# Audio tower on one core: the token stage with all its turns by transposing transfers and three convolution banks, and another order inside an attention slot

## Chip, core, metric

One core of a Trainium2 chip runs the whole program in one launch. The metric is the device time of that core in microseconds (us), the median of several executions. The engines named here: TensorE (PE, with its weight loads PEld), VectorE (DVE), ScalarE (ACT), GpSimd (POOL) and SyncE (SP), which here only issues transfers.

## What is computed

Three stages follow each other. The token stage makes 2048 tokens of 1024 numbers (16 tiles of 128 channels), the attention stage adds a 32-head latent attention to them, and the feed-forward stage adds a linear layer with a low-rank expert part.

```python
h = conv1d(x, conv_in_w, pad=3)                    # x (16, 64, 2048), 7 taps, 128 channels
h = gelu(groupnorm1(h))
h = conv1d(h, dw_w, stride=2, pad=2, groups=128) + dw_b   # 5 taps for each channel
h = conv1d(h, pw_w)                                # 128 x 128, one tap
h = gelu(groupnorm1(h))                            # 16 tiles of 128 x 1024

n = layernorm(h)
q_c = rmsnorm(n @ w_qa, g_qa)                      # 384 latents for the queries
kv  = n @ w_kva                                    # 128 latents and 64 rope numbers
k_c, k_rope = rmsnorm(kv[:, :128], g_kva), rope(kv[:, 128:])
q = q_c @ w_qb                                     # 32 heads, 128 + 64 (rope) each
p = softmax(q . [k_c @ w_kvb_key, k_rope] * scaling)     # 128 x 128 in each tile and head
h = h + (p @ (k_c @ w_kvb_value)) @ w_o

h = h + layernorm(h) @ W_base.T + b_base + experts(layernorm(h))
```

Every product wants float32 accuracy and runs in float16: an operand is split into a high half and a low half, and a product is three products (high by high, high by low, low by high). So each operand costs one pass for the high half (mostly ACT) and one for the low half (mostly DVE, "value minus high half").

## The kernel before

**Token stage** (`token_phase`, lines 108 to 640). The work is written out engine by engine: each engine runs its own list in order, and semaphores join them. A function `body(i, p, ok)` is the list of one iteration; a tile b passes through five iterations, and `AHEAD, MID, HID, PROJ, TAIL = -2, 1, 2, 3, 4` say by how many iterations each step trails the convolution of its tile. In iteration i:

- PE: convolution piece 0 of tile i (12 products of 512 columns into one of two banks `conv_ps`); the statistics product (`stat_ps`, L609), which spreads the group norm sums of tile i-1 (first norm) and tile i-2 (second norm) over the partitions; transposes of the normalised tile i-3 (`turn_ps`, L569) between the convolution pieces 1, 2 and 3; the projection of tile i-3 to q and kv in two pieces; transposes of the latents of tile i-4 (L631, L633, L640); the pointwise product of tile i-1 (`pw_ps`).
- ACT: copies of the four convolution pieces to `y1`, high halves of the turned tile (`ht_h`), the first gelu (`g1`, L261) of tile i-1, the second gelu (`resid`), the float16 copy of input tile i+2 (`x_high`), squares for the rms norm, high halves of the latents, the normalised tile `hid` (L303).
- DVE: sums for the second group norm (`bn2`, L479) at the head of the iteration, the copy of the statistics (`s`, L485), the latents' first steps, low halves of the turned tile, the sums of the first norm (`bn1`, L403), the five taps of the depthwise convolution (`dw`, L419 and L423, five instructions over SBUF alone), the sums of the layer norm (`bn3`), the low halves of the latents out of `turn_ps`.
- POOL: eleven short linked steps that turn `s` into the scale and bias `c12` of both group norms (L337 to L344), then the rms scales of tile i-4, the layer norm scales of tile i-2, and last the low half of input tile i+2 (`x_low`, L326).
- SP: the input loads.

The cycle through an iteration is: statistics product (PE), `s` (DVE), group norm steps (POOL), first gelu (ACT), taps (DVE), sums of `bn1` and `bn2` (DVE), next statistics product.

**Attention stage** (`attention_phase`, lines 706 to 1119) has 32 rounds of one group of four heads and one of two halves of the tokens, four slots (128-token tiles) in each: 128 slots. Slot s = 4t + j does on PE: scores (`s_ps`, L1051 to L1058, the rope part from `zt`), latents of the slot before (`av_ps`, L1093 to L1095, from the turned probabilities `turned`), the rope queries of the next slot, the queries of the next round (`qp_ps`), in slots 1 to 3 one of three pieces of a weight product (`prod_ps`, "products", which the last rounds don't have), and the outputs of the slot before (`out_ps`, 24 products of 512 columns). The softmax chain of a slot runs beside: maxima (DVE, `mx`), exponentials (ACT, L851), reciprocal and normalisation (DVE), high half (ACT) and low half (DVE) into `halves`, one transposing transfer by SP into `turned`. SP issues the rope turn `zt` of slot s+1 ahead of `turned` of slot s. The next heads' weights (928 KB) are loaded by ACT's queue at the head of its round's list (L819); ACT comes to that line when it has taken slot 3 of the round before.

**Feed-forward stage** (`ffn_phase`, from line 1126): not touched.

## Time and profile before

| what | value |
| --- | --- |
| median of 3 runs | 2093.45 us (2093.0 to 2094.6) |
| the profiled execution: its own time | 2096.29 us |
| its span | 2094.5 us |
| token stage | 0.7 to 458.9 us |
| attention stage | 458.9 to 1857.9 us |
| feed-forward stage | 1857.9 to 2094.5 us |
| PE busy over the span | 1924.3 us (92%) |
| DVE, ACT, POOL busy | 1310.3, 755.6, 286.4 us |

Busy shares over the span mix three stages with different limits, so they are to be read stage by stage. PE's busy time is modelled and runs a little over into the next product; where it stands in a window at nearly the whole window, PE does not wait. POOL works only in the token stage and beside the feed-forward stage.

### The profile page before, as it was taken

The page shows a single profiled execution, that of the slowest core. Times are in us where ns is not written, and L with a number is a line of the kernel's source. Part 1 is how long each engine was busy: PE and PEld are TensorE (multiplying, and loading weights), DVE is VectorE, ACT ScalarE, POOL GpSimd, SP SyncE. Part 2 cuts the span into 40 slices and gives each one's busy share as a digit, 9 for nine tenths or more (in the row PEclk, how much of TensorE's full clock was granted, in tenths as well). Part 3 has the DMA queues.
Part 4 walks back from the last instruction along what each step waited for, and adds up shares of the span by engine and source line. Part 5 has one row for each costly group of instructions (what it writes and reads, how often), then busy time and mean ns, then how long its engine had stood idle before and what let it go on. Part 6 is the DMA issues. An engine that isn't in the chain of part 4 may idle for free. (4 is left out here: it accounts for less than half of the span.)

```text
span 2094.5 us, 33517 instructions
## 1 busy us (share of the span) xinstructions
PE 1924.3 (92%) x11794; PEld 1064.8 (51%) x11794; DVE 1310.3 (63%) x2805; ACT 755.6 (36%) x2051; POOL 286.4 (14%) x612
## 2 busy tenths in 40 slices
PE   4788888768999999999999999999999999959999
PEld 1344445444555555555555555555555555525554
DVE  2667677635666666666566665666666666665554
ACT  3444544324333333333333333333333333332221
POOL 2355554320000000000000000000000000023332
PEclk9899999879999999999999999999999999989999
DMA  5112211002332232222322223222232212243332
GB/s 139 41 41 50 53 41 39 19 26 73 75 57 57 57 63 63 55 57 57 75 57 56 54 55 73 56 57 57 66 58 57 39 38 44 41 134 81 82 81 71
DMA packets 250668, 125.27 MB, mean 60 GB/s; under 512 B 240272, under 2 KB 240528, under 8 KB 248336
## 3 DMA queue, kind: packets, MB, share of 16 engines
q1 hardware_dynamic: 246192, 94.71, 21.7%
q10 hardware_dynamic: 4320, 28.51, 4.4%
q8 instruction: 94, 1.54, 0.3%
q14 instruction: 62, 0.51, 0.1%
HBM read 56.07 MB, written 8.39 MB: 31 GB/s over the span
## 5 line engine op out<-in xcount | busy, mean ns | idle before, releaser
L1073 PE MATMUL out_ps<-m_h,ot_h 128*128 128x512 f16 x1024 | 388.2, 379 | 4.1 <-DVE ot_l L872 4.1
L1075 PE MATMUL out_ps<-m_h,ot_l 128*128 128x512 f16 x1024 | 388.1, 379 | 0.0
L1074 PE MATMUL out_ps<-m_l,ot_h 128*128 128x512 f16 x1024 | 388.1, 379 | 0.0
L922 DVE SCALAR_TENSOR_TENSOR resid<-out_ps,resid 128x512 f32<-128x512 f32 x256 | 177.0, 691 | 285.4 <-PE out_ps L1075 281.4
L787 ACT ACTIVATE ot_h<-av_ps 128x512 f16<-128x512 f32 x128 | 76.4, 597 | 744.2 <-PE av_ps L1095 744.2
L1264 POOL MEMSET fpower<- 128x1 f32 x1 | 0.1, 99 | 1405.0 <-POOLq L706 1405.0
L851 ACT ACTIVATE prob<-s_ps,nmx 128x128 f32<-128x128 f32 x512 | 180.1, 372 | 5.7 <-DVE nmx L948 5.7
L1073 PEld LDWEIGHTS out_ps<-m_h,ot_h 128*128 128x128 f16 x1024 | 100.2, 98 | 129.7 <-issue 13.4
L1074 PEld LDWEIGHTS out_ps<-m_l,ot_h 128*128 128x128 f16 x1024 | 100.2, 98 | 129.2 <-issue 18.6
L1075 PEld LDWEIGHTS out_ps<-m_h,ot_l 128*128 128x128 f16 x1024 | 100.2, 98 | 120.9
L943 DVE TENSOR_REDUCE mx<-s_ps 128x4 f32<-128x512 f32 x128 | 88.5, 691 | 74.8 <-PE s_ps L1058 74.8
L872 DVE SCALAR_TENSOR_TENSOR ot_l<-av_ps,ot_h 128x512 f16<-128x512 f32 x128 | 88.5, 691 | 70.3 <-ACT ot_h L787 70.3
L872 DVE SCALAR_TENSOR_TENSOR halves<-prob,halves 128x512 f16<-128x512 f32 x128 | 88.6, 692 | 46.4 <-ACT halves L787 46.4
L851 ACT ACTIVATION_READ_ACCUMULATOR prob<-s_ps,nmx 128x1 f32 x512 | 109.3, 213 | 0.0
L1008 PE MATMUL qp_ps<-qct_h,wp_h 128*128 128x512 f16 x378 | 104.8, 387 | 0.0
L1008 PE MATMUL qp_ps<-qct_h,wp_l 128*128 128x512 f16 x378 | 102.7, 381 | 0.0
L1008 PE MATMUL qp_ps<-qct_l,wp_h 128*128 128x512 f16 x378 | 102.1, 379 | 0.0
L787 ACT ACTIVATE halves<-prob 128x512 f16<-128x512 f32 x128 | 80.6, 630 | 51.3 <-DVE prob L956 51.3
L1377 PE MATMUL fout<-wb_l,fht_h 128*128 128x512 f16 x256 | 97.3, 380 | 0.0
L1377 PE MATMUL fout<-wb_h,fht_h 128*128 128x512 f16 x256 | 97.3, 380 | 0.0
L1377 PE MATMUL fout<-wb_h,fht_l 128*128 128x512 f16 x256 | 97.1, 379 | 0.0
L1051 PE MATMUL s_ps<-kct_h,qp_h 128*128 128x128 f16 x512 | 92.4, 219 | 0.4 <-DVE qp_l L872 0.4
(239 smaller groups left out, 4011.7 us busy)
## 6 DMA issues: line engine op xcount, KB each, us to landing
wide<-heads_in ACTq DMA_DIRECT2D x30, 928.0 KB, 5.3
wide<-x_in SPq DMA_DIRECT2D x32, 512.0 KB, 6.3
tower_out<-result SPq DMA_DIRECT2D x16, 512.0 KB, 2.6
stage<-wb_in SPq DMA_DIRECT2D x8, 512.0 KB, 8.5
resid<-wqk_in SPq DMA_DIRECT2D x1, 2304.0 KB, 12.5
zt<-z SPq DMA_TRANSPOSE x128, 2.4
turned<-halves SPq DMA_TRANSPOSE x128, 3.0
wide<-heads_in SPq DMA_DIRECT2D x2, 928.0 KB, 5.3
```

The lines of the kernel that those rows point to most:

```text
L787: act.activation(out, src, ACT.Copy, scale=scale).then_inc(done, 1)
L851: act.activation(prob[:, h, :], s_ps[:, h * P:(h + 1) * P], ACT.Exp, bias=nmx[:, h:h + 1], scale=EXP_SCALE, accum_out=rsum[:, h:h + 1]).th ...
L872: dve.scalar_tensor_tensor(out=out, in0=src, scalar=scale, in1=high, op0=ALU.mult, op1=ALU.subtract).then_inc(done, 1)
L922: dve.scalar_tensor_tensor(out=resid[:, at], in0=out_ps[hf][:, :], scalar=1.0 / (O_S * M_S), in1=resid[:, at], op0=ALU.mult, op1=ALU.add). ...
L943: dve.tensor_reduce(mx[:, :], s_ps[:, :].rearrange("p (h n) -> p h n", h=HEADS), AX.X, ALU.max).then_inc(max_step, 1)
L1008: last = pe.matmul(bank[:, :], w[:, bass.ds(side, 1), k, j, :].rearrange("p a n -> p (a n)"), q[:, k, bass.ds(tok, CHUNK)], start=n == 0, ...
L1051: pe.matmul(out[h], q_h[h], k_h, start=h == 0, stop=False)
L1073: pe.matmul(out_ps[hf][:, :], ot_h[:, h, :], m_h[:, at], start=h == 0, stop=False)
L1074: pe.matmul(out_ps[hf][:, :], ot_h[:, h, :], m_l[:, at], start=False, stop=False)
L1075: last = pe.matmul(out_ps[hf][:, :], ot_l[:, h, :], m_h[:, at], start=False, stop=h == HEADS - 1)
L1264: pool.memset(power[:, :], -0.5).then_inc(powered, 1)
L1377: pe.matmul(out_ps[p][hf][:, :], h[p][:, k, :], w[:, k, hf * CHUNK:(hf + 1) * CHUNK], start=k == 0 and n == 0, stop=False)
```

## The change

In the token stage:

- The lags become -1, 1, 2, 3, 4 and a sixth, LOW = 5; there is one iteration more.
- PE makes no transposes. ACT writes the normalised tile and its high half to SBUF (`hid2`), DVE the low half beside it, and SP turns both with one transposing transfer of 128x2048 into `ht`. The latents are treated alike: high halves by ACT (iteration TAIL), low halves by DVE one iteration later (LOW), then two transposing transfers by SP (128x1024 into `lat`, 128x256 into the same).
- The freed bank is a third convolution bank, and the projection is one piece behind convolution piece 3.
- `bn2` and its aggregation move from the head of the next iteration to the end of DVE's list. `bn3` stands ahead of the last two `bn1` sums.
- POOL computes the low half of input tile i+1 right behind the group norm steps, instead of tile i+2 behind the layer norm steps. ACT's high half of that tile stands between copies 0 and 1.
- The first input tile is loaded head first (1032 columns), and the convolution of its first two pieces waits for the head alone.
- The rms scales take seven linked steps, not eight; the group norm's eleven steps lose one wait.

In the attention stage the latents product of slot s moves to the end of slot s itself, and the outputs of slot s-1 to before the queries. SP issues `zt` of slot s behind `turned` of slot s-1. ACT's and DVE's halves of `av_ps` stand at the end of the slot, and the output additions of DVE ahead of the queries' low halves. The heads' loads keep their place at the head of ACT's round.

The core of the diff:

```diff
-    AHEAD, MID, HID, PROJ, TAIL = -2, 1, 2, 3, 4
+    AHEAD, MID, HID, PROJ, TAIL, LOW = -1, 1, 2, 3, 4, 5
-        conv_ps = [pb("conv_ps0"), pb("conv_ps1")]
-        stat_ps, turn_ps = pb("stat_ps"), pb("turn_ps")
+        conv_ps = [pb("conv_ps0"), pb("conv_ps1"), pb("conv_ps2")]
+        stat_ps = pb("stat_ps")
...
+                if ok(PROJ):
+                    b = i - PROJ
+                    sp.wait_ge(hid_lo, b + 1)
+                    need(sp, proj_done, b, B)
+                    sp.dma_start_transpose(ht[:, :, :], hid2[:, :]).then_inc(hid_turned, 16)
+                if ok(LOW):
+                    b = i - LOW
+                    sp.wait_ge(lat_lo, b * 2 + 2)
+                    sp.dma_start_transpose(lat[:, 0:8, b * P:(b + 1) * P],
+                                           lat2[:, :, :].rearrange("p a n -> p (a n)")).then_inc(lat_turned, 16)
...
             def body(i, p, ok):
-                if isinstance(i, int) and i == 0:
-                    x_low(1, 1)
                 if ok(MID) or ok(HID):
                     group_norms(i)
+                if ok(AHEAD) and i >= 0:
+                    x_low(i - AHEAD)
                 if ok(TAIL):
                     latent_scales(i - TAIL)
                 if ok(HID):
                     layer_norm(i - HID)
-                if ok(AHEAD) and (not isinstance(i, int) or i >= 0):
-                    x_low(i - AHEAD, p)
...
+                if ok(PROJ):
+                    b = i - PROJ
+                    dve.wait_ge(hid_hi, b + 1)
+                    need(dve, hid_turned, b * 16, B * 16)
+                    low(hid2[:, D:2 * D], hid[:, :], LN_S, hid2[:, 0:D], hid_lo)
+                if ok(LOW):
+                    latents_low(i - LOW)
                 if ok(TAIL):
                     take_latents(i - TAIL)
-                if ok(PROJ):
-                    hidden_low(i - PROJ, 0)
...
             def turn_rope(s):
-                wait_apart(sp, sp_passed, (z_lo, s + 1))
+                waits = [(z_lo, s + 1)]
...
             turn_rope(0)
-            turn_rope(1)
             turn_prob(0)
-            with sp.Fori(1, ROUNDS * QUAD - 1) as s:
-                turn_rope(s + 1)
+            with sp.Fori(1, ROUNDS * QUAD) as s:
+                turn_rope(s)
                 turn_prob(s)
...
                     scores(now, j, operands)
-                    if behind[0]:
-                        latents(*behind)
...
+                    pe.wait_ge(p_turned, s * 16 + 16)
+                    pe.matmul(av_ps[:, :], kc[:, at], probs_h, start=True, stop=False)
+                    pe.matmul(av_ps[:, :], kc[:, at_l], probs_h, start=False, stop=False)
+                    pe.matmul(av_ps[:, :], kc[:, at], probs_l, start=False, stop=True).then_inc(av_done, 1)
```

POOL in the token stage, around the input's low half (`x_l`), before: it closes the iteration, behind the layer norm scales (`ly`, `lc`) and ahead of the next group norms (`msq`, `gv`, `gy`).

```order
L105 TENSOR_TENSOR ly<-ly,lt 128x1
L368 TENSOR_TENSOR lc<-st,ly 128x1
L369 TENSOR_SCALAR lc<-lc 128x1
L326 TENSOR_TENSOR x_l<-wide 128x2054
L337 TENSOR_TENSOR msq<-s 128x2
L338 TENSOR_TENSOR msq<-s,msq 128x2
```

And after:

```order
L355 TENSOR_TENSOR c<-yg,gt 128x2
L356 TENSOR_TENSOR msq<-s,c 128x2
L357 TENSOR_TENSOR c<-params,msq 128x2
L335 TENSOR_TENSOR x_l<-wide 128x2054
L366 TENSOR_SCALAR rv<-ss 128x2
L367 TENSOR_TENSOR ry<-rv,half 128x2
```

The low half has moved from ahead of the group norm steps to right behind them, where the rms scales (`rv`, `ry`) now follow it.

DVE in the token stage, from the sums of the layer norm (`bn<-resid`) to the statistics of the second norm, before: these are the first norm's last sums (`bn<-y`), the low halves of the latents, and the second norm's sums (`bn<-pw_ps`).

```order
L510 BN_STATS bn<-resid 128x6 x2
L516 BN_AGGR st<-bn 128x2
L403 BN_STATS bn<-y_0 128x6
L410 BN_AGGR st<-bn 128x2
L411 SCALAR_TENSOR_TENSOR st<-st 128x1
L394 SCALAR_TENSOR_TENSOR qct_l<-turn_ps,qct_h 128x3x128
L394 SCALAR_TENSOR_TENSOR kct_l<-turn_ps,kct_h 128x128
L394 SCALAR_TENSOR_TENSOR kc_l<-k_n,kc_h 128x128
L394 SCALAR_TENSOR_TENSOR kr_l<-turn_ps,kr_h 128x128
L479 BN_STATS bn<-pw_ps 128x6 x2
L410 BN_AGGR st<-bn 128x2
L411 SCALAR_TENSOR_TENSOR st<-st 128x1
```

And after:

```order
L441 SCALAR_TENSOR_TENSOR dw<-g,params,dw 128x1024 x4
L513 BN_STATS bn<-resid 128x6 x2
L519 BN_AGGR st<-bn 128x2
L523 RECIPROCAL rinv<-nrm 128x2
L421 BN_STATS bn<-y_1 128x6 x2
L428 BN_AGGR st<-bn 128x2
L429 SCALAR_TENSOR_TENSOR st<-st 128x1
L536 BN_STATS bn<-pw_ps 128x6 x2
L428 BN_AGGR st<-bn 128x2
L429 SCALAR_TENSOR_TENSOR st<-st 128x1
L490 COPY s<-stat_ps 128x4
L412 SCALAR_TENSOR_TENSOR hid_hl<-hid,hid_hl 128x1024
```

The latents' low halves are gone from between the two norms' sums, the five taps (`dw`) stand right ahead of this piece, and the statistics copy (`s`) is followed by the low half of the normalised tile (`hid_hl`), which has only SBUF operands.

PE in the attention stage, between two score products (`s_ps`) of a slot with a weight product, before: `av_ps` are the latents, `rope_ps` the rope queries, `qp_ps` the queries, `prod_ps` the weight product, `out_ps` the outputs.

```order
L1058 MATMUL s_ps<-kr_l,zt 128x128
L1093 MATMUL av_ps<-turned,kc_h 128x512
L1094 MATMUL av_ps<-turned,kc_l 128x512
L1095 MATMUL av_ps<-turned,kc_h 128x512
L1024 MATMUL rope_ps<-wr_h,qct_h 128x256 x3
L1024 MATMUL rope_ps<-wr_l,qct_h 128x256 x3
L1024 MATMUL rope_ps<-wr_h,qct_l 128x256 x3
L1008 MATMUL qp_ps<-qct_h,wp_h 128x512 x3
L1008 MATMUL qp_ps<-qct_h,wp_l 128x512 x3
L1008 MATMUL qp_ps<-qct_l,wp_h 128x512 x3
L992 MATMUL prod_ps<-wide 128x128 x3
L1073 MATMUL out_ps<-m_h,ot_h 128x512
```

And after:

```order
L1031 MATMUL out_ps<-m_h,ot_h 128x512
L1032 MATMUL out_ps<-m_l,ot_h 128x512
L1033 MATMUL out_ps<-m_h,ot_l 128x512
L966 MATMUL qp_ps<-lat,wp_h 128x512 x3
L966 MATMUL qp_ps<-lat,wp_l 128x512 x3
L966 MATMUL qp_ps<-lat,wp_h 128x512 x3
L950 MATMUL prod_ps<-wide 128x128 x3
L1071 MATMUL av_ps<-turned,kc 128x512
L1072 MATMUL av_ps<-turned,kc 128x512
L1073 MATMUL av_ps<-turned,kc 128x512
L1009 MATMUL s_ps<-lat,qp_h 128x128
```

The latents have gone from behind the scores of the next slot to the end of their own slot, ahead of the next scores.

## Rows read from the trace of the kernel before

**Rows 1.** Windows: us, busy and instructions of each engine, granted clock, DMA share, GB/s.

```profile
0.70:66.00 65.30, 32.61 (x115) 12.94 (x115) 27.60 (x30) 21.94 (x22) 17.84 (x19) 0.87 0.48 126
66.00:420.50 354.50, 293.92 (x1639) 165.28 (x1639) 238.32 (x489) 163.24 (x263) 174.41 (x401) 0.97 0.16 39
420.50:458.90 38.40, 24.13 (x138) 17.03 (x138) 13.73 (x50) 10.14 (x27) 11.24 (x43) 0.72 0.00 1
528.30:1692.30 1164.00, 1143.66 (x7291) 639.32 (x7290) 753.46 (x1620) 423.88 (x1404) 0.00 (x0) 1.00 0.28 58
```

**Rows 2.** Timeline, token iteration 8: start, duration, engine, line, operation, count [idle before, releaser].

```profile
227.89 1.28 DVE L479 BATCH_NORM_STATS2 bn<-pw_ps 128x6 f32<-128x512 f32 x2
...
230.36 0.36 PE L609 MATMUL stat_ps<-st,mean_mat 128*128 128x4 f32 x2 [2.71 <-issue]
...
231.12 0.19 POOL L337 TENSOR_TENSOR msq<-s 128x2 f32<-128x2 f32 x1 [0.88 <-DVE s L485]
...
235.69 2.10 ACT L261 ACTIVATE g<-y,c 128x2048 f32<-128x2048 f32 x1 [0.77 <-POOL c L344]
...
238.66 5.25 DVE L423 SCALAR_TENSOR_TENSOR dw<-g,params,dw 128x1024 f32<-128x1024 f32 x4
```

**Rows 3.** Timeline, token iteration 1: POOL, DVE and ACT around `x_l` of tile 2.

```profile
37.80 4.07 POOL L326 TENSOR_TENSOR x_l<-wide 128x2054 f16<-128x2054 f32 x1 [9.42 <-ACT wide L226]
...
38.14 0.69 DVE L403 BATCH_NORM_STATS2 bn<-y 128x6 f32<-128x512 f32 x1 [7.72 <-ACT y L232]
...
39.19 3.90 DVE L394 SCALAR_TENSOR_TENSOR wqk_l<-resid,wqk_h 128x1152 f16<-128x1152 f32 x1 [0.36 <-ACT wqk_h L220]
...
41.83 1.30 POOL L337 TENSOR_TENSOR msq<-s 128x2 f32<-128x2 f32 x1
...
48.61 2.09 ACT L261 ACTIVATE g<-y,c 128x2048 f32<-128x2048 f32 x1 [6.61 <-POOL c L344]
```

**Rows 4.** Tile view, feed-forward stage: shortest/median/longest ns of a low half from SBUF.

```profile
L1271 DVE SCALAR_TENSOR_TENSOR hid_l<-hid,hid_h x16: 1171/1224/1226, 1868.1 to 2071.0; 128x1024 f16<-128x1024 f32 x16
```

**Rows 5.** Timeline, attention slot 49 (j = 1): scores, latents, softmax chain, next maxima.

```profile
1013.78 0.22 PE L1051 MATMUL s_ps<-kct_h,qp_h 128*128 128x128 f16 x1
...
1014.89 0.38 PE L1093 MATMUL av_ps<-turned,kc_h 128*128 128x512 f16 x1
...
1015.10 0.69 DVE L943 TENSOR_REDUCE mx<-s_ps 128x4 f32<-128x512 f32 x1 [0.43 <-PE s_ps L1058]
...
1016.24 0.36 ACT L851 ACTIVATE prob<-s_ps,nmx 128x128 f32<-128x128 f32 x1
...
1017.51 0.23 ACT L851 ACTIVATION_READ_ACCUMULATOR prob<-s_ps,nmx 128x1 f32 x1
...
1018.37 0.69 DVE L956 TENSOR_TENSOR prob<-prob,rrec 128x512 f32<-128x512 f32 x1
...
1019.76 0.69 DVE L872 SCALAR_TENSOR_TENSOR halves<-prob,halves 128x512 f16<-128x512 f32 x1 [0.36 <-ACT halves L787]
...
1025.63 0.69 DVE L943 TENSOR_REDUCE mx<-s_ps 128x4 f32<-128x512 f32 x1 [0.42 <-PE s_ps L1058]
```

**Rows 6.** Timeline, DVE: maxima of three following slots (j = 3, 0, 1) without loads.

```profile
1682.93 0.69 DVE L943 TENSOR_REDUCE mx<-s_ps 128x4 f32<-128x512 f32 x1 [0.42 <-PE s_ps L1058]
...
1693.66 0.69 DVE L943 TENSOR_REDUCE mx<-s_ps 128x4 f32<-128x512 f32 x1 [0.42 <-PE s_ps L1058]
...
1703.53 0.69 DVE L943 TENSOR_REDUCE mx<-s_ps 128x4 f32<-128x512 f32 x1 [0.42 <-PE s_ps L1058]
```

**Rows 7.** Page, part 6: DMA issues, KB each, median us from issue to landing.

```profile
wide<-heads_in ACTq DMA_DIRECT2D x30, 928.0 KB, 5.3
...
turned<-halves SPq DMA_TRANSPOSE x128, 3.0
```

**Rows 8.** Waits of PE, 528.3 to 1692.3 us: us in all, times, longest.

```profile
PE s_ps L1057 <- DMA zt<-z: 10.2, 13, 1.7
PE av_ps L1093 <- DMA turned<-halves: 9.5, 28, 0.4
```

More of the change, by code:

```diff
@@ L186, in _, with load @@
         @block.sync
         def _(sp):
-            def load(b):
-                sp.dma_start(x_f[0:CI, PAD:PAD + T], x_d[bass.ds(b, 1), :, :].rearrange("a c t -> (a c) t")
-                             ).then_inc(x_loaded, 16)
-                sp.dma_start(x_f[CI:P, PAD - 1:PAD - 1 + T],
-                             x_d[bass.ds(b, 1), :, :].rearrange("a c t -> (a c) t")).then_inc(x_loaded, 16)
+            def load(b, lo, hi, done):
+                xs = x_d[b:b + 1, :, :].rearrange("a c t -> (a c) t")
+                for rows, pad in ((slice(0, CI), PAD), (slice(CI, P), PAD - 1)):
+                    at = slice(max(lo - pad, 0), min(hi - pad, T))
+                    sp.dma_start(x_f[rows, at.start + pad:at.stop + pad], xs[:, at]).then_inc(done, 16)
@@ L561, in conv @@
                 last.then_inc(conv_done, 1)
-            def turn_hidden(b, hf):
-                if hf == 0:
-                    pe.wait_ge(hid_done, b + 1)
-                    need(pe, t2_lo, b - 1, B)
-                need(pe, ht_lo, b * 2 + hf, 2 * B)
-                for k in range(4):
-                    last = pe.transpose(turn_ps[:, k * P:(k + 1) * P],
-                                        hid[:, (4 * hf + k) * P:(4 * hf + k + 1) * P], ident)
-                last.then_inc(ht_done, 1)
             def pointwise(b):
@@ L844, in body @@
                     s = now.slot + j
-                    if before or j:
-                        latent_high(now.slot + (j - 1), not before and j == 1)
                     act.wait_ge(max_step, s * 2 + 2)
@@ L863, in body @@
                         prod_high(now.t + HEADS, now.parity, now.side * -1 + 1, now.place, j - 1, prod_ps, False)
-                if not after:
-                    latent_high(now.slot + (QUAD - 1), False)
+                    act.wait_ge(av_done, s + 1)
+                    if before or j:
+                        act.wait_ge(out_done, s * 2)
+                    high(ot_h[:, :, :].rearrange("p h n -> p (h n)"), av_ps[:, :], O_S / (PR_S * KC_S), o_hi)
             rounds(act, start, body)
@@ L940, in body @@
                     s = now.slot + j
-                    behind = (now, j - 1) if j else (before, QUAD - 1)
                     dve.wait_ge(s_done, s + 1)
@@ L958, in body @@
                                       ).then_inc(norm_step, 1)
+                    behind = (now, j - 1) if j else (before, QUAD - 1)
                     if after or j < QUAD - 1:
@@ L968, in body @@
                         prod_low(now.t + HEADS, now.parity, now.side * -1 + 1, now.place, j - 1, prod_ps)
-                    if behind[0]:
-                        add_out(*behind, 0)
-                        add_out(*behind, 1)
+                    dve.wait_ge(o_hi, s + 1)
+                    low(ot_l[:, :, :].rearrange("p h n -> p (h n)"), av_ps[:, :], O_S / (PR_S * KC_S),
+                        ot_h[:, :, :].rearrange("p h n -> p (h n)"), o_lo)
                 if not after:
-                    latent_low(now.slot + (QUAD - 1))
                     for hf in range(2):
@@ L1084, in start @@
                 rope(Round(pe, 0), 0)
-            def latents(r, j):
-                if not r.known or r.t or j:
-                    pe.wait_ge(o_lo, r.slot + j)
-                at = bass.ds(r.tok + j * P, P)
-                probs_h, probs_l = (turned[:, at, :].rearrange("p h n -> p (h n)")
-                                    for at in (slice(0, HEADS), slice(HEADS, 2 * HEADS)))
-                pe.wait_ge(p_turned, r.slot * 16 + (16 * j + 16))
-                pe.matmul(av_ps[:, :], kc_h[:, at], probs_h, start=True, stop=False)
-                pe.matmul(av_ps[:, :], kc_l[:, at], probs_h, start=False, stop=False)
-                pe.matmul(av_ps[:, :], kc_h[:, at], probs_l, start=False, stop=True).then_inc(av_done, 1)
             def body(before, now, after, more):
@@ L1410, in build @@
         with ExitStack() as first_two:
[L1411 to L1412 removed]
+            keep.update(make(first_two, [("lat", (P, 2 * (QT + 1) + 2, TOK), F16), ("kc", (P, 2 * TOK), F16)]))
             keep.update(make(first_two, [(f"wide{i}", (P, XW), F32) for i in range(2)]))
```

435 lines of the change are left out of this document (203 added, 232 removed).

## Prediction

> **What bounds the kernel now.** I read the windows by stage first, since the shares over the span mix stages. In attention rounds 1 to 27 PE is busy for 1143.7 of 1164.0 us at full clock [rows 1]: that stage is bound by PE. In the token stage's steady part (from the statistics product of iteration 2 to that of 17, 15 periods of 354.5/15 = 23.6 us) PE is busy for 19.6 us a period, and no other engine comes near the whole. So there I followed one cycle through the timeline of iteration 8 [rows 2]: statistics product 230.36, first POOL step 231.12, first gelu 235.69, taps from its end at 237.79 to 243.91, and so back to the next statistics product. An iteration is as long as that closed loop, wherever PE idles. The reader is to see in rows 3 that two engines hold each other up over SBUF, in rows 5 the length of the softmax chain, in rows 6 a slot bound by PE alone. The feed-forward stage isn't touched.
>
> The profiled execution ran 2096.29 us with a span of 2094.5; the median is 2093.45. I work out differences in us and take them from the median, 2.8 us less than that execution.
>
> **Token stage, steady period.** The loop after, from statistics product to statistics product:
> - to the first POOL step .76 [rows 2], as before;
> - group norm 235.69 - 231.12 = 4.57, less one wait (a step of .19 is followed by some .19 until the next): 4.4;
> - gelu 2.10; from its end to the end of the taps 238.66 + 5.25 - 237.79 = 6.12;
> - after the taps, on DVE: three pairs of sums (layer norm, last two of the first norm, second norm), each 1.28 like the pair at 227.89 [rows 2]: 3.84. From the last pair's end to the statistics product before it was 230.36 - 229.17 = 1.19, of which the held step (below) is .45, so .75; two shorter aggregations and a reciprocal ahead, about .65 and .45. In all 5.7.
>
> Sum 19.1. The low halves of the latents, which stood in this piece, and PE's transposes leave the loop.
>
> Two costs come in, both seen at iteration 1 [rows 3]. While POOL computed `x_l` (37.80 to 41.87), DVE's `wqk_l`, an instruction with only SBUF operands, took 3.90 us for what is else 1.3, and ended 1.2 us after `x_l`. While `wqk_l` ran on, POOL's `msq` took 1.30 instead of .19. I read: each waits for the other's instruction.
> - **x_l behind group norm.** It starts some .2 behind the gelu's start, ends 4.07 later, and the taps are ready 2.1 behind the gelu's start: they wait about 2.0. Before, `x_l` stood at the iteration's end. Bound: 0 (no hold) to 4.
> - **hid_l and the latents' low halves** stand right behind the statistics copy, while POOL starts its group norm steps. A low half of 128x1024 from SBUF takes 1.22 [rows 4]; the three of the latents, 640 columns together in three instructions, about 1.1 by the same rate and a start each. POOL can slip a step in between: I take 1.8 of 2.3. Bound: 0 to 2.3.
> - PE waits some 3 us for the pointwise product's input in each iteration, and its clock falls in such gaps (0.97 of full in the steady part, 0.72 in the drain [rows 1]): .3.
>
> Period 19.1 + 2.0 + 1.8 + .3 = 23.2. Iterations at the edges lack a part: 21.1 for the first (no low halves yet), 22.3 for the next two, ten at 23.2, 20.9 without `x_l`, 20.5 without convolution: 339.1 against 354.5, **-15.5**.
>
> The turns by transfer: `hid` goes in one 128x2048 transfer. A turn of 128x1024 takes 3.0 [rows 7], so one of twice the size takes 3.0 to 6.0; I take 4.5. PE needs it behind convolution pieces 1 to 3, which are 36 products of 512 columns: twenty score products of 128 columns take 1014.89 - 1013.78 = 1.11 [rows 5], so a product of 512 columns takes .22, and the pieces 7.9. DVE has the low half 2 us behind the statistics product, and 5.9 are left: the convolution hides the turn. Without that cover a us more would first use up PE's gap of 3 ahead of the pointwise product, and then show in full. Cost 0. The latents' turns have a whole iteration. On SP all three stand ahead of the next input's load, which waits for `x_l` anyway.
>
> **Start.** Before, `x_l` of tile 2 stood ahead of the first group norm on POOL: the first statistics copy was done 7.72 ahead of 38.14 [rows 3], at 30.4, but the steps began at 41.83. After, they begin at once, end near 35, and the gelu waits only for ACT's `x_high` of tile 2 (done at 37.6, since POOL's `x_l` was released by it at 37.80): about 37 instead of 48.61, -11.6. The head load brings about 1 more, since input 1 waits for the same weight transfers: **-12.5** at iteration 2.
>
> **Drain.** One iteration more, in which turn, projection, squares, scales and the two latent turns follow each other with nothing beside them: two transfers of 3 (+6) and no transposes on PE (-1): **+5** on 38.4 [rows 1].
>
> Token stage: **-23**.
>
> **Attention.** Slots without a weight product take 9.87 (1703.53 - 1693.66), slots 2 and 3 10.73 (1693.66 - 1682.93) [rows 6], slot 1 10.53 [rows 5]: a round of 41.87. Rounds 1 to 27 would take 1130.5 at that and took 1164.0. Where they lose: PE waits for `zt` 10.2 us and for `turned` 9.5 [rows 8], about one slot with `zt` in every second round. These are the slots in which the heads' load of 928 KB is under way (5.3 us to landing [rows 7]) and the turns then take up to twice their usual time. Its place: ACT came to it in slot 3, about when that slot's turns go out. After, ACT ends each slot with the halves of `av_ps`, so it comes to the load early in slot 0, and it lands ahead of that slot's turns. I take this loss as gone: it is the stage's gain.
>
> The price is the chain, which must now end in its own slot. From rows 5: maxima to the first exponential .93 when ACT is free (1.14 there), exponentials to 1017.74 1.50, reciprocal and handovers .28, normalisation to the end of the low half 1020.45 - 1018.37 = 2.08, SP .2, transfer 3.04, to PE .14: 8.17, and .06 as maxima wait for the low half of `av_ps` behind which they now stand. PE wants the latents 1.97 ahead of the next maxima (three products of 512 columns .65, score products 1.11, and 1015.10 - 1014.89 = .21 of handover): at 7.90 in slot 0, 8.57 in slot 1, 8.76 in slots 2 and 3. So only slot 0 waits, .33, and .1 for its new operands: 42.3 a round, 27 x 42.3 = 1142.1, **-21.9**. In rounds 28 to 31 no slot has a weight product, and there is no load: 12 slots at 10.35 instead of 9.87, **+5.8**; the last round, chain-bound, about +2.5, less .9 in the tail: **+1.6**. Round 0: its first slot waits for its own chain instead of going on, a slot of 8.2 + 1.97 = 10.2 with few products of its own to fill it, and a lower clock behind that, **+4**. Late turns: in 28 of 108 slots PE waited for `turned` before, though it then had a slot's scores more [rows 8]; I count one in twelve late by 1.5 with half a slot in hand: **+8**. Attention: **-2.5**.
>
> **Sum:** 2093.45 - 23 - 2.5 = 2068. Its own range, from the bounds above (the two holds between half of 3.8 and their full 4.3 over some twelve iterations, -23 to +6; late turns 0 to 16; start and drain 3 each way): 2048 to 2088.
>
> The Trainium skill ("VectorE: DVE Perf Modes", section "The three transpose paths") gives 1309 ns for a 128x128 block through the transposing transfer and 390 ns on TensorE, which speaks against this change. Here 128x1024, eight such blocks, landed in 3.0 [rows 7], and by the page it would be 10.5: the trace disagrees. By the page the turn of `hid`, sixteen blocks, would take an estimated 20.9 (rival 4 is that rule as a mechanism).
>
> **Rivals.**
> 1. *The holds don't bite.* `x_l` and taps, or low halves and POOL steps, run side by side. For: what I saw is one place, at iteration 1. Against: both directions show there. Then the period is 19.4: ten iterations gain 3.8 each, two 2.9, the three at the edges some 2 together, 46 more: 2022.
> 2. *A turn comes later than before (slower).* After, `zt` goes out right behind `turned`, and both land in the last third of the slot. For: turns grow with other traffic. Against: the two overlapped before too (SP issued them in the order `zt`, `turned`, so `turned`'s 3.0 holds whatever `zt` in front of it costs). With x us more on `turned`: x in each of 27 slots 0 and 15 late slots, x - .34 in slots 1 and x - .53 in slots 2 and 3: at x = .6 it is 25 + 7 + 4 = 36, more than the 25.5 gained, so it turns the sign from x = .5; at 1.0 it is 42 + 18 + 25 = 85, 2153, at .6 2104. Centre 2115.
> 3. *More holding.* Every low half holds the whole group norm, or the clock falls to its lower level (1.2 GHz) behind the gap in all iterations: period 24.3, +16: 2084.
> 4. *The turn of `hid` is much slower than the line through the small turns says*, as a transfer that goes block by block, with others on its queue. It passes PE's slack at 5.9 + 3 = 9 us, three times a turn of half its size; at 12 (four times) the period grows by 3 to 26.2, the token stage loses 12 x 3 = 36, and the time is 2104. Against: rows 7, with a turn of half the size at 3.0.
>
> **How the numbers follow.** My forecast .55, rival 1 .13, rival 2 .14, rival 3 .15, rival 4 .03. About 4 us (0.2%) can be told from no change. The forecast is faster in 19 of 20 (.52), rival 1 wholly (.13), rival 3 in 8 of 10 (.12): .77. Their remainders (.06) and the near end of rival 2 (.02) lie within .2%: .08. The rest of rival 2 and rival 4 are slower: .15. Range: left out are the lower half of rival 1 (.06), rival 2 beyond x = .55 (.1) and most of rival 4 (.02): 2022 to 2100.
>
> **What will show it.** Period of the statistics products 23.2 (19.4 for rival 1); taps with a first instruction of near 2.8 instead of .81 beside `x_l`; `msq` or `gv` near 1.3 beside `hid_l`; first gelu near 37; `hid`'s turn 4 to 5 us; the token stage's end near 436. In attention: rounds of 42.3, waits for `turned` in slot 0 alone, .3 each; none for `zt`; the heads' load at slot 0's start. It is wrong if `turned` takes over 3.5 in most slots, if the load still meets the turns, or if the statistics product waits for PE's own work instead of DVE.

## The result and the profile after

The changed kernel takes 2043.74 us (2042.18 to 2045.04) against 2094.02 before (2093.0 to 2100.72), a ratio of 0.9751 [0.9733, 0.9768] over all executions: 50 us faster by the medians, where 26 were forecast. Its profiled execution has a span of 2042.9 us, 51.6 under that of before. The windows of after, cut at the same events as [rows 1], with the same columns:

```profile
0.70:57.02 56.32, 29.87 (x114) 12.48 (x115) 25.71 (x31) 19.64 (x21) 11.27 (x18) 0.88 0.51 130
57.02:375.55 318.53, 270.06 (x1423) 140.72 (x1422) 242.84 (x433) 160.88 (x237) 201.13 (x388) 0.95 0.38 82
375.55:422.16 46.61, 18.56 (x104) 12.55 (x105) 12.56 (x42) 11.14 (x23) 13.12 (x42) 0.68 0.27 51
494.25:1631.16 1136.91, 1136.74 (x7292) 632.76 (x7291) 761.31 (x1620) 442.73 (x1405) 0.00 (x0) 1.00 0.26 60
```

Stage by stage, from the timelines of both (the token stage is cut at the statistics products of iterations 2 and 17 and at the first score product, the attention stage at the first maxima of a round):

| piece | before, us | after, us | change | forecast |
| --- | --- | --- | --- | --- |
| start, to iteration 2 | 65.96 | 57.02 | -8.9 | -12.5 |
| 15 steady periods | 354.4 | 318.5 | -35.9 | -15.5 |
| drain, to the first scores | 40.0 | 46.6 | +6.6 | +5 |
| round 0 | 41.4 | 45.4 | +4.0 | +4 |
| rounds 1 to 27 | 1163.8 | 1136.9 | -26.9 | -21.9 + 8 for late turns |
| rounds 28 to 30 | 118.4 | 123.2 | +4.8 | +5.8 |
| last round to the end | 282.4 | 287.2 | +4.8 | +1.6 |

Two pieces hold what was missed: the steady periods (20 us) and rounds 1 to 27 (13 us). The other pieces came out some 7 us worse than forecast, which hides a part of it. Token iteration 8 of after in the timeline (columns as in [rows 2]; L335 is `x_l`, L412 the low half of the normalised tile, L350 the pow step of the group norm, L437 the first tap):

```profile
206.72 0.35 PE L599 MATMUL stat_ps<-st,mean_mat 128*128 128x4 f32 x2 [0.80 <-issue]
207.48 0.19 POOL L347 TENSOR_TENSOR msq<-s 128x2 f32<-128x2 f32 x1 [1.33 <-DVE s L490]
208.55 1.23 DVE L412 SCALAR_TENSOR_TENSOR hid_hl<-hid,hid_hl 128x1024 f16<-128x1024 f32 x1 [1.28 <-ACT hid_hl L275]
208.68 1.68 POOL L350 TENSOR_TENSOR gy<-gv,half 128x2 f32<-128x2 f32 x1 [0.18 <-POOL gv L349]
213.00 4.10 POOL L335 TENSOR_TENSOR x_l<-wide 128x2054 f16<-128x2054 f32 x1
213.08 2.10 ACT L288 ACTIVATE g<-y,c 128x2048 f32<-128x2048 f32 x1 [1.79 <-POOL c L357]
215.21 2.44 DVE L437 TENSOR_SCALAR dw<-g,params 128x1024 f32<-128x1024 f32 x1 [1.99 <-ACT g L288]
217.69 5.25 DVE L441 SCALAR_TENSOR_TENSOR dw<-g,params,dw 128x1024 f32<-128x1024 f32 x4
226.34 1.29 DVE L536 BATCH_NORM_STATS2 bn<-pw_ps 128x6 f32<-128x512 f32 x2
228.36 0.36 PE L599 MATMUL stat_ps<-st,mean_mat 128*128 128x4 f32 x2 [0.80 <-issue]
```

Both forecast holds are there: the tap takes 2.44 us instead of .81 while `x_l` runs to 217.10, and POOL's pow step 1.68 instead of .72 while DVE's low half runs. From the first group norm step to the gelu it is 5.60 instead of 4.4. But this period is 21.64, not 23.2, and the ten periods from iteration 5 to 14 have a mean of 21.68 (120.12 to 336.87).

The loop of these ten periods, piece by piece (means from the timelines, us):

| piece of the loop | before | after | after, forecast |
| --- | --- | --- | --- |
| statistics product to POOL's first step | .76 | .74 | .76 |
| group norm on POOL, to the gelu | 4.60 | 5.50 | 4.4 + 1.8 |
| gelu | 2.10 | 2.10 | 2.10 |
| gelu's end to the taps' end | 6.14 | 7.62 | 6.12 + 2.0 |
| taps' end to the next statistics product (the tail) | 10.29 | 5.72 | 5.7 + .3 |
| period | 23.89 | 21.68 | 23.2 |

So the gain is the tail's, 4.6, less 2.4 for the two holds. Most of the tail's gain is a wait of DVE before the change, for a high half of the latents (`kr_h`) that stood behind `hid` in ACT's list; with the latents' halves in another iteration it is gone. This is read from the two timelines: no run takes these steps apart. In iteration 8 of before:

```profile
251.93 0.29 DVE L394 SCALAR_TENSOR_TENSOR kr_l<-turn_ps,kr_h 128x128 f16<-128x128 f32 x1 [3.14 <-ACT kr_h L308]
...
254.36 0.36 PE L609 MATMUL stat_ps<-st,mean_mat 128*128 128x4 f32 x2 [2.72 <-issue]
```

After, the tail is 5.43 in six of the ten periods and 6.16 in the other four (iterations 5, 7, 11 and 14). In each of the four the granted clock of TensorE fell to 0.5 (1.2 GHz) for 3.4 us, .3 to 1.4 us behind the end of PE's wait for the taps. The pointwise product then takes up to 3.54 instead of 1.98, the convolution piece behind it is late, and the statistics product waits for that piece. Iteration 5: the window of the low clock (columns as in [rows 1]), and the pointwise product there and in iteration 8:

```profile
136.68:140.09 3.41, 3.41 (x5) 0.99 (x5) 3.03 (x9) 1.94 (x7) 1.68 (x7) 0.50 0.01 2
```

```profile
136.40 3.54 PE L570 MATMUL pw_ps<-dw,pw 128*128 128x512 f32 x4 [2.25 <-DVE dw L441]
...
222.99 1.98 PE L570 MATMUL pw_ps<-dw,pw 128*128 128x512 f32 x4 [2.24 <-DVE dw L441]
```

Attention, first slot of round 1, and its neighbours (ACT's load, the two turns of SP, PE's latents, DVE's maxima):

```profile
494.43 0.33 ACTq L788 DMA_DIRECT2D wide<-heads_in  x1
495.61 0.68 DVE L900 TENSOR_REDUCE mx<-s_ps 128x4 f32<-128x512 f32 x1
500.46 1.23 SPq L745 DMA_TRANSPOSE turned<-halves  x1
502.14 1.19 SPq L737 DMA_TRANSPOSE zt<-z  x1
503.65 0.38 PE L1071 MATMUL av_ps<-turned,kc 128*128 128x512 f16 x1
505.74 0.68 DVE L900 TENSOR_REDUCE mx<-s_ps 128x4 f32<-128x512 f32 x1
537.73 0.68 DVE L900 TENSOR_REDUCE mx<-s_ps 128x4 f32<-128x512 f32 x1
```

The chain takes 503.65 - 495.61 = 8.04 (forecast 8.23), slot 0 is 10.13, a round 537.73 - 495.61 = 42.12 (forecast 42.3), and all 27 are within .05 of that. The load goes out 6 us ahead of the turn. In the waits of PE over these rounds no turn appears any more [rows 8].

### The profile page after: what moved, and what is told of

Read it like the earlier page. It is cut to its first block and busy times, and to the rows that moved or that the text cites. A ratio compares the mean times of both kernels' runs of the same rounds, so it can differ in the third digit from the quotient of the medians.

```text
span 2042.9 us, 32412 instructions
## 1 busy us (share of the span) xinstructions
PE 1892.5 (93%) x11538; PEld 1029.6 (50%) x11538; DVE 1321.2 (65%) x2742; ACT 773.2 (38%) x2020; POOL 308.4 (15%) x596
## 5 line engine op out<-in xcount | busy, mean ns | idle before, releaser
L756 ACT ACTIVATE qp_h<-qp_ps 128x512 f16<-128x512 f32 x126 | 75.3, 597 | 492.6 <-PE qp_ps L966 492.6
L835 DVE SCALAR_TENSOR_TENSOR qp_l<-qp_ps,qp_h 128x512 f16<-128x512 f32 x126 | 87.2, 692 | 234.5 <-ACT qp_h L756 234.5
L966 PE MATMUL qp_ps<-lat,wp_h 128*128 128x512 f16 x756 | 205.6, 381 | 0.0
L982 PE MATMUL rope_ps<-wr_h,lat 128*128 128x256 f16 x768 | 127.8, 276 | 0.0
L966 PEld LDWEIGHTS qp_ps<-lat,wp_h 128*128 128x128 f16 x756 | 74.4, 98 | 90.9 <-issue 2.3
L812 ACT ACTIVATION_READ_ACCUMULATOR prob<-s_ps,nmx 128x1 f32 x512 | 103.8, 203 | 0.0
L966 PE MATMUL qp_ps<-lat,wp_l 128*128 128x512 f16 x378 | 102.6, 381 | 0.0
L582 PE MATMUL q_ps<-wqk_h,ht 128*128 128x384 f16 x256 | 78.7, 342 | 24.5 <-DMA ht<-hid_hl 24.5
```

Of the source, the lines that this page charges most:

```text
L582: pe.matmul(q_ps[:, 0:QR], lhs, w[:, k, 0:QR], start=first, stop=end)
L756: act.activation(out, src, ACT.Copy, scale=scale).then_inc(done, 1)
L812: act.activation(prob[:, h, :], s_ps[:, h * P:(h + 1) * P], ACT.Exp, bias=nmx[:, h:h + 1], scale=EXP_SCALE, accum_out=rsum[:, h:h + 1]).th ...
L835: dve.scalar_tensor_tensor(out=out, in0=src, scalar=scale, in1=high, op0=ALU.mult, op1=ALU.subtract).then_inc(done, 1)
L966: last = pe.matmul(bank[:, :], w[:, bass.ds(side, 1), k, j, :].rearrange("p a n -> p (a n)"), q[:, k, bass.ds(tok, CHUNK)], start=n == 0, ...
L982: last = pe.matmul(rope_ps[:, 0:HEADS * RD], q[:, k, bass.ds(tok + j * P, P)], w[:, bass.ds(side, 1), k, :].rearrange("p a n -> p (a n)"), ...
```

## Experiments

The theories: *holds* (in the steady token period two holds of about 1.2 and 1.6 us lie in series in the loop, and nothing else of size), and *load* (the attention stage's gain is that the heads' load no longer meets the turns; the order inside the slot has no gain of its own). Their rivals: another wait or PE takes the holds' place; the order itself gains. A total without a range is of one execution. The kernel before took 2098 to 2101 us (medians) beside these runs and 2094 beside the changed kernel, so totals compare to some 5 us; periods and rounds are read from the traces.

### The holds, one by one and together

```diff
-                pool.tensor_tensor(x_l[p][:, :], x_f[:, :], x_h[p][:, :], ALU.subtract).then_inc(x_lo, 1)
+                n = XW if b < 2 else 64
+                pool.tensor_tensor(x_l[p][:, 0:n], x_f[:, 0:n], x_h[p][:, 0:n], ALU.subtract).then_inc(x_lo, 1)
```

> The changed kernel, with POOL's x_l of tiles 2 to 15 over 64 of 2054 columns only (the rest of the low half is left out). Theory of the hold: the first tap instruction falls from 2.44 us to .81, the steady period from a mean of 21.2 to about 19.7, stage and total 20 us shorter, about 2023 us. Rival, PE or another wait takes the hold's place (PE has 18 to 19 us of its own work in a period, so it can't): under 5 us gained. Rival, the tap is long for another reason: it stays at 2.4.

```diff
-                low(lat2[:, 1, 0:QR], q_g[:, :], rinv[:, 0:1], lat2[:, 0, 0:QR], lat_lo)
+                n = QR if b < 1 else 64
+                low(lat2[:, 1, 0:n], q_g[:, 0:n], rinv[:, 0:1], lat2[:, 0, 0:n], lat_lo)
...
-                    low(hid2[:, D:2 * D], hid[:, :], LN_S, hid2[:, 0:D], hid_lo)
+                    n = D if b < 1 else 64
+                    low(hid2[:, D:D + n], hid[:, 0:n], LN_S, hid2[:, 0:n], hid_lo)
```

> The changed kernel, with DVE's low half of the normalised tile and of the query latents over 64 columns only from the second tile on (the rest of these low halves is left out). Theory of the hold: the group norm on POOL, first step to gelu, falls from 5.60 us to about 4.4 (its pow step from 1.68 to .72), the period by 1.2, the total by some 14 us to 2030. Rival, POOL's steps are this long for their own sake: no change in period or total (within 4 us).

Both edits at once:

> The changed kernel with both reductions at once: x_l of tiles 2 to 15 over 64 columns, the low halves of the normalised tile and of the query latents over 64 columns from the second tile on (the rest of these low halves is left out). Theory, the two holds lie in series in the loop: period 21.2 less 1.3 less 1.1, near 18.9, total near 2000 us. Rival, behind one of them another limit comes up (PE's own work, some 18.5 us a period with the gap ahead of the pointwise product): period not under 19.6.

Timelines: the tap and two statistics products with the small `x_l`; the pow step and two statistics products with the small low halves; two statistics products with both.

```profile
201.88 0.81 DVE L438 TENSOR_SCALAR dw<-g,params 128x1024 f32<-128x1024 f32 x1 [1.99 <-ACT g L288]
...
193.38 0.35 PE L600 MATMUL stat_ps<-st,mean_mat 128*128 128x4 f32 x2 [0.80 <-issue]
...
213.41 0.36 PE L600 MATMUL stat_ps<-st,mean_mat 128*128 128x4 f32 x2 [0.80 <-issue]
```

```profile
200.51 0.72 POOL L350 TENSOR_TENSOR gy<-gv,half 128x2 f32<-128x2 f32 x1 [0.18 <-POOL gv L349]
...
198.56 0.36 PE L601 MATMUL stat_ps<-st,mean_mat 128*128 128x4 f32 x2 [0.80 <-issue]
...
218.95 0.36 PE L601 MATMUL stat_ps<-st,mean_mat 128*128 128x4 f32 x2 [0.80 <-issue]
```

```profile
205.97 0.36 PE L602 MATMUL stat_ps<-st,mean_mat 128*128 128x4 f32 x2 [0.40 <-issue]
...
225.01 0.35 PE L602 MATMUL stat_ps<-st,mean_mat 128*128 128x4 f32 x2 [0.68 <-issue]
```

Total 2020.48, 2022.67 and 2000.13 us. Means of the ten periods from iteration 5 to 14: 20.03 without `x_l`, 20.31 without the low halves, 18.81 without both, against 21.68. So taking out one gains 1.65 or 1.37, both 2.87: they lie in series, and the loop without holds is 18.8. The tap is .81 and the pow step .72 again. That the edit also shortens DVE's own list is not the gain: in the changed kernel DVE waits 1.99 us for the gelu behind that list.

The two single gains add up to 3.02 and not to 2.87 because something else goes with either hold. In none of the three runs does the clock fall in these ten periods, and the tail is 5.43 throughout, .29 less in the mean. The pieces of the loop have the holds alone: gelu's end to the taps' end 7.62 less 6.13 is 1.49 for `x_l`, the group norm 5.50 less 4.41 is 1.09 for the low halves; with the .29 that is 2.87.

### `x_l` in other places

Behind the layer norm steps on POOL, as before the change:

```diff
                     group_norms(i)
-                if ok(AHEAD) and i >= 0:
-                    x_low(i - AHEAD)
...
                     layer_norm(i - HID)
+                if ok(AHEAD) and i >= 0:
+                    x_low(i - AHEAD)
```

> The changed kernel with x_l last on POOL, behind the layer norm steps, where it stood before (for the tile of the next iteration). Theory: the tap is free (.81), but the 4.1 us of x_l now stand ahead of the next group norm, which starts some 2.8 us later than its statistics: period 21.2 - 1.6 + 2.8 = 22.4, total about 2060 us. Rival, x_l costs the same wherever it stands: 21.2.

2104.26 us, a period of 26.7: far more than expected. The timeline (POOL, DVE, PE, and ACT's next input) has why:

```profile
126.22 3.82 POOL L335 TENSOR_TENSOR x_l<-wide 128x2054 f16<-128x2054 f32 x1
126.52 3.54 DVE L429 SCALAR_TENSOR_TENSOR st<-st 128x1 f32<-128x1 f32 x1
130.10 1.89 PE L561 MATMUL conv_ps<-x_l,wc_h 128*128 128x512 f16 x4 [4.93 <-POOL x_l L335]
131.78 0.43 PE L599 MATMUL stat_ps<-st,mean_mat 128*128 128x4 f32 x2
...
137.29 1.92 ACT L255 ACTIVATE wide<-wide 128x2054 f16<-128x2054 f32 x1 [4.67 <-DMA wide<-x_in]
```

I had costed it as a delay of POOL's next steps alone. But the lag of this input is now one iteration, so piece 0 of the next convolution wants `x_l` at once, and the statistics product stands behind that piece on PE: all 3.8 us are in the loop. PE idles 4.93 for it, and the granted clock is 0.5 from 128.0 to 134.8 us, so the products that wait for `x_l` take 1.89 instead of 1.02. Beside `x_l` even a step on one column per partition was held, 3.54 us instead of .22. So the tail is 10.5 instead of 5.7. The rest is in the group norm, 7.2 to the gelu instead of 5.5: the next input's load waits for `x_l`, and ACT waits 4.67 for that input and takes it ahead of the gelu. The low lag fits only where `x_l` is early.

On DVE, behind the second sum of the first norm (POOL's `x_low` goes):

```diff
+                if ok(AHEAD) and i >= 0:
+                    b = i - AHEAD
+                    dve.wait_ge(x_hi, b + 1)
+                    dve.tensor_tensor(x_l[b % 2][:, :], x_f[:, :], x_h[b % 2][:, :], ALU.subtract
+                                      ).then_inc(x_lo, 1)
                 if ok(MID):
                     for k in range(DW_TAPS):
```

> The changed kernel with x_l of tiles 1 to 15 on DVE instead of POOL, behind the second sum of the first norm, in the 2 us in which DVE waits for the gelu. Theory of the hold: x_l takes 2.30 there, the taps start .3 to .4 late instead of 1.6, period 20.0 to 20.2, total 2024 to 2030 us. Rival, DVE as the bound gets longer by the instruction: period 21.2 + .7 or more, 2050 us.

2029.54 us (2028.0 to 2030.73), 0.9678 [0.9654, 0.9702] of the kernel before, period 20.15. The timeline: the gelu on ACT, `x_l` and the first tap on DVE.

```profile
206.34 2.10 ACT L288 ACTIVATE g<-y,c 128x2048 f32<-128x2048 f32 x1 [1.78 <-POOL c L352]
206.41 2.28 DVE L502 TENSOR_TENSOR x_l<-wide 128x2054 f16<-128x2054 f32 x1
208.61 0.81 DVE L430 TENSOR_SCALAR dw<-g,params 128x1024 f32<-128x1024 f32 x1
```

It fills the time in which DVE waited for the gelu, and the tap is free: 14 us. Here too the clock doesn't fall in the ten periods, so the 14 us include the .29 a period as well.

### Where the attention stage's gain lies

The kernel before, with its load later:

```diff
                     act.wait_ge(prod_done, now.t * 3 + 3 * HEADS)
                     act.wait_ge(wr_lo, now.t + HEADS)
+                    if now.t:
+                        act.wait_ge(p_turned, now.slot * 16)
                     load(now.t + HEADS + 1, 1 - now.parity)
```

> The kernel before, with one wait ahead of the heads' load: it is issued when the turn of the last slot of the round has landed, so about 4 us later. Theory, the loss of rounds 1 to 27 is this load's meeting with the two turns: no late zt and turned, rounds of 41.9 to 42.0 instead of 43.1, 27 to 30 us gained, about 2066 us. Rival, the new order inside the slot makes the gain: no change, 2094 within 4 us.

2066.09 us (2062.8 to 2069.68), 0.9852 [0.9826, 0.9878] of the kernel before, which took 2097.96 beside it. The maxima that open rounds 1 and 2, and PE's waits over rounds 1 to 27 (columns as in [rows 8]):

```profile
530.48 0.69 DVE L945 TENSOR_REDUCE mx<-s_ps 128x4 f32<-128x512 f32 x1 [0.42 <-PE s_ps L1060]
...
572.34 0.69 DVE L945 TENSOR_REDUCE mx<-s_ps 128x4 f32<-128x512 f32 x1 [0.42 <-PE s_ps L1060]
```

```profile
PE av_ps L1095 <- DMA turned<-halves: 1.0, 3, 0.5
```

Rounds of 41.86 (the 27 have a mean of 41.92) instead of 43.1, and waits of 1.0 us instead of 19.7 [rows 8]: one wait in the old order brings 31.9 us in rounds 1 to 27, where the whole change brings 26.9, at no cost in the rounds around them (41.1 us in round 0, 118.4 in rounds 28 to 30).

Then the load nearer to the turn in the changed kernel, three times. First in slot 3, ahead of the halves of `av_ps`:

```diff
+                    if after and j == QUAD - 1:
+                        next_heads(after)
                     act.wait_ge(av_done, s + 1)
```

(`next_heads` holds the two waits and the load that stood at the head of the round's list.)

> The changed kernel, with the heads' load issued on ACT in slot 3 ahead of the halves of av_ps, where it stood before, about half a us behind the issue of that slot's turn. Theory of the load's place: the turn of slot 3 takes 4.5 to 6.5 us instead of 3.04, PE waits for it, rounds of 43.5 to 45 instead of 42.1, 2080 to 2120 us. Rival, the order alone makes the gain: rounds stay at 42.1, 2044 us.

2041.44 us, rounds of 42.11. This did not test it: in the new slot the weight product and its halves come late, so ACT got to the load 8.9 us into slot 3 and not at 5.4, when the turn had landed. Next behind `rope_high` in slot 0 (the lines at the head of the round go, here and in the run after it):

```diff
                         rope_high(s + 1)
+                    if j == 0 and more and now.t + HEADS + 1 < NH:
+                        act.wait_ge(prod_done, now.t * 3 + 3 * HEADS)
+                        act.wait_ge(wr_lo, now.t + HEADS)
+                        load(now.t + HEADS + 1, 1 - now.parity)
```

> The changed kernel with the heads' load issued in slot 0 behind the rope query's high half, some 2 us ahead of that slot's turn. Theory, load and turn meet and the new slot has nothing in hand: the turn of slot 0 takes 5 to 6 us, slot 0 12 us instead of 10.1, rounds near 44, total 2085 to 2105 us. Rival, the new order is robust against the load: rounds stay at 42.1.

2042.79 us: the load goes out 2.5 us ahead of the turn, which then takes 3.2 in the median and 3.74 at most; rounds are 42.1 to 42.8, with a mean of 42.3. I expected far too much for that distance. Last, the same lines a step later, behind the high half of the probabilities:

```diff
                     high(p_h, prob[:, :, :].rearrange("p h n -> p (h n)"), PR_S, p_hi)
+                    if j == 0 and more and now.t + HEADS + 1 < NH:
...
+                        load(now.t + HEADS + 1, 1 - now.parity)
```

> The changed kernel with the heads' load issued in slot 0 behind the high half of the probabilities, so just ahead of the issue of that slot's turn (in the run before it went out 2.6 us ahead, and the turns took 3.04 to 3.74). Theory, what counts is that the turn goes out while most of the load's packets are still queued: the turn of slot 0 takes about 5.3 us as it did in the kernel before, slot 0 12.3 us, rounds 44.3, total near 2100 us. Rival, a load costs a turn under .7 us wherever it lies: rounds of 42.2 to 42.6, total under 2058 us.

2079.14 us. The timeline of ACT, SP and DVE and PE's waits:

```profile
491.96 0.68 DVE L900 TENSOR_REDUCE mx<-s_ps 128x4 f32<-128x512 f32 x1
...
495.41 0.34 ACTq L788 DMA_DIRECT2D wide<-heads_in  x1
...
496.81 1.23 SPq L745 DMA_TRANSPOSE turned<-halves  x1
...
503.29 0.68 DVE L900 TENSOR_REDUCE mx<-s_ps 128x4 f32<-128x512 f32 x1
...
535.28 0.68 DVE L900 TENSOR_REDUCE mx<-s_ps 128x4 f32<-128x512 f32 x1
```

```profile
PE av_ps L1071 <- DMA turned<-halves: 38.6, 26, 1.9
```

At 1.4 us the turn takes 4.25 to 4.95. Slot 0 of round 1 takes 11.33 and that round 43.3; rounds 1 to 27 have a mean of 43.5. That is a little less than the 5.3 and 44.3 expected; before, a rope turn was in flight with load and turn, which may be why, but no run shows it. The theory of the load holds, and the new order isn't proof against it.

### The order of SP's turns

```diff
             turn_rope(0)
+            turn_rope(1)
             turn_prob(0)
-            with sp.Fori(1, ROUNDS * QUAD) as s:
-                turn_rope(s)
+            with sp.Fori(1, ROUNDS * QUAD - 1) as s:
+                turn_rope(s + 1)
                 turn_prob(s)
+            turn_prob(ROUNDS * QUAD - 1)
```

> The changed kernel with SP's old order: the rope turn of slot s+1 is issued ahead of the turn of the probabilities of slot s. The three kernels with that order and the late load had some ten turns of 3.3 to 4.9 us each, in the same slots, and the changed kernel has none. Theory, the late turns come with the two turns going out one right behind the other in this order: about ten late ones again, each costing up to 1.3 us in the new slot, total 5 to 12 us over the changed kernel, 2049 to 2056 us. Rival, they come from something else in the old slot: none late, 2044 us within 3.

```profile
PE av_ps L1071 <- DMA turned<-halves: 12.5, 27, 0.7
```

No late turn, so that theory falls; yet 2062.2 us, so its rival's number fails too. Issuing one transposing transfer takes SP 1.2 us (the rows of attention above), and `turned` now goes out behind that, .46 us later in the slot: slot 0 takes 10.57 instead of 10.12, and so do slots 1 and 2 in the rounds without a weight product. Putting `zt` behind `turned` is a part of the change that the shorter chain needs; I had costed it at nothing in either direction. What makes some ten turns of the old slot order 3.2 to 4.9 us long, always in the same slots (12, 23, 36, 47, ...) and never in the new, stays open; behind the late load they cost PE 1.0 us in all. The traces name a suspect: in the three kernels with that order and the late load, each of the 30 long turns has a packet of 16 KB on the queue of instruction loads (q8) that starts between .7 us ahead of its issue and 2.9 behind, and in the changed kernel no turn has one. But four turns of other runs had one right at their issue and took 3.03 to 3.05, and no run moves these packets. In the DMA view of the turn of slot 23 below (the next kernel, 693.7 to 698.5 us):

```profile
q8 instruction: 1, 0.02, 2.1%
```

### A better version

The changed token stage, the old order in the slot (on all engines) with the late load, and then `x_l` on DVE as well, as above:

```diff
                     scores(now, j, operands)
+                    if behind[0]:
+                        latents(*behind)
...
+                    if now.t:
+                        act.wait_ge(p_turned, now.slot * 16)
                     load(now.t + HEADS + 1, 1 - now.parity)
```

> The changed token stage with the order of the attention stage before, and there the heads' load issued behind the landing of the last slot's turn. Theory, the new order gains only by where the load falls and costs its chain in each slot without a weight product: rounds 1 to 27 41.86 instead of 42.1 (-6.5), rounds 28 to 30 39.5 instead of 41.05 (-4.7), round 0 41.1 instead of 45 (-4), the last round -3.5, total 19 us under the changed kernel, about 2024 us. Rival, the new order gains something of its own: not under 2036 us.

> As the kernel with the old order in a slot and the late load, and in the token stage x_l of tiles 1 to 15 on DVE behind the second sum of the first norm. The stages follow each other, so the gains add: 14 us less again, about 2010 us. Rival, the earlier end of the token stage costs the attention prologue what it gains: 2024 us.

2025.88 us (2025.26 to 2027.93), 0.9667 [0.965, 0.9684], and 2013.2 us (2010.07 to 2014.36), 0.9605 [0.9589, 0.9622]: rounds of 41.9, and the gains nearly add (17.9 and 12.7 us here, 14.2 for `x_l` on DVE alone). The new order gains nothing of its own: it costs these 18 us. The second beats both kernels, by 30 us the changed one.

## Why the prediction was too small

The steps that failed are sizes, and one double count. In the token sum the two holds, 2.0 + 1.8 a period, measured 1.49 + 1.09, and the tail of 5.7 measured 5.43. In the attention sum the +8 for late turns measured 0, and slot 0 lost .25 instead of .43. The holds were seen as named; the late turns did not come.

- **Bounds and loop: right.** The token loop ran through the same chain, and PE's transposes left it at no cost. `hid`'s turn landed in 4.3 us (forecast 4.5), .6 ahead of the projection; rival 4 is out. The Trainium skill ("VectorE: DVE Perf Modes", section "The three transpose paths") gives 1309 ns for one 128x128 block through a transposing transfer. Taken once for each block it doesn't hold here: sixteen blocks landed in 4.3 us.
- **The holds: right in kind, too large.** `x_l` starts .08 ahead of the gelu and not .2 behind, so 1.92 of it are left at the gelu's end (217.10 - 215.18), and the tap lost 1.63 of these; where `x_l` takes 3.82, in every other period, it lost 1.35. For the low halves I let POOL lose 1.8 of 2.3; it loses 1.09, nearly all in the pow step. The Trainium skill ("SBUF — State Buffer", section "🔬 SBUF: two separate sides") says that VectorE and GpSimd take one pair of ports in turn, each for a whole instruction, where VectorE reads two SBUF operands or runs in a two-port mode. Here the trace agrees in the main: the tap ends .55 us behind `x_l`, and alone it takes .81.
- **The tail of 5.7: a little large; .3 for the clock: right.** The tail is 228.36 - 222.94 = 5.4, since the reciprocal runs beside the sums. The clock's falls, .73 in four of ten periods, cost .29 in the mean. The .3 was not worked out from a row, so its closeness is luck; that PE's wait and the clock behind it lengthen the period was right. One reading was wrong: before the change PE's wait of some 3 us stands ahead of the statistics product [rows 2] and not of the pointwise product, where it stands after. With .5, .7 and .3 less, 23.2 is 21.7. The short first and last periods, costed by the same holds, make the other 5 us.
- **Late turns: the step that failed in attention.** I took PE's 28 waits for `turned` in [rows 8] as a rate of late turns that would go on. The late load shows that nearly all of them were the load's (19.7 us to 1.0), which I had already counted as gone: +8 was a cost counted against a gain of the same cause. (Beside the load `turned` took 4.8 to 6.9 us before and `zt` 5.4 to 7.4, so up to three times their usual time, not twice.) Slot 0 and the chain were right within .2 us, which over 27 rounds is the other 5.
- **Start: 3.6 us too much.** Seen in the timeline of ACT at iteration 1:

```profile
37.09 1.92 ACT L255 ACTIVATE wide<-wide 128x2054 f16<-128x2054 f32 x1 [4.97 <-DMA wide<-x_in]
...
39.38 1.15 ACT L242 ACTIVATE wqk_h<-resid 128x1152 f16<-128x1152 f32 x1
40.56 1.28 ACT L288 ACT_TABLE_LOAD   x1
41.85 2.09 ACT L288 ACTIVATE g<-y,c 128x2048 f32<-128x2048 f32 x1
```

  I had the gelu at 37, right behind the input's high half, and left out the weights' quarter and the table load that stand between them on ACT. The head load brought little: input 2 is there no earlier. A part is this execution's: in the five other kernels with the same token stage iteration 2 came at 54.4 to 55.4 us, not 57.0.
- **Drain and last round:** +6.6 and +4.8 for +5 and +1.6; in the drain PE waits 17.3 us for `ht` in two waits:

```profile
PE q_ps L582 <- DMA ht<-hid_hl: 17.3, 2, 9.0
```

  In the last round three slots take 31.5 us instead of 28.1: the chain costs 3.4 there where I took 2.5.
- **The range.** Its upper end, 2088, adds up the bounds as listed (6, 8, 3 and 3). Its lower end does not: 23, 8, 3 and 3 below 2068 is 2031, not 2048, and the measured time lies above that.
- **Rivals.** Rival 1 (no hold) is out as it stood, though the time lies nearer to it than to the forecast's. Rival 2 is out: with `zt` issued right behind it `turned` took 3.02 to 3.16 in all 128 slots. It is a load put on the turn that lengthens it. Rival 3 (more holding, a period of 24.3) is out by the period. The side was right, the size half.

## What to carry to other kernels

When a transfer that others wait for is late in a part of its instances, look at what else is issued just ahead of it: here one wait ahead of the neighbour's issue was worth some 30 us, more than a new order of the whole stage. Taking out one hold can take another cost with it: look at the pieces of the loop, not only at its length. A gain and a penalty read from the same row must not both go into the sum. An instruction that holds another engine is best put where that engine's own queue waits for something else, or on that engine itself.

## What the runs showed of the hardware

- A transposing transfer from SBUF of 128x512 landed in 2.4 us, of 128x1024 in 3.0, of 128x2048 in 4.3; the 128x1024 one issued 2 us behind that of 128x2048 took 3.7.
- Issued 1.4 us behind a direct load of 928 KB, the 128x1024 one took 4.3 to 5.0 us; 2.5 us behind it, 3.0 to 3.7; 6 us behind it, 3.0.
- A POOL instruction of 3.8 us on two SBUF operands kept a DVE step on one column per partition for 3.54 us instead of .22.
- In the attention stage SP takes 1.2 us to issue a transposing transfer, in the token stage 1.3 to 1.9, and the next one behind it waits for that.
- In four of ten token periods the granted clock fell to 0.5 for 3.4 us behind a wait of PE of 2.0 to 2.25 us, and the pointwise product took 2.5 to 3.5 us instead of 1.98; behind the same wait in iteration 8 it did not fall.
